# A gated Mamba and feed-forward layer on one core: a new order of five engines' work, softplus's own table, and idle transposes in the first batch

## The reference

```python
# xattn part, per batch
x  = einsum('bld,ed->bel', ctx, in_proj_w)          # 256 channels x 256 tokens
u  = silu(causal_conv4(x, conv_w) + conv_b)
dt_low, Bm, Cm = split(einsum('bdl,ed->bel', u, x_proj_w), [8, 24])
dt = softplus(einsum('brl,dr->bdl', dt_low, dt_proj_w) + dt_proj_b)
A  = -exp(A_log)                                     # 256 channels x 16 states
for each token: state = state * exp(dt * A) + (dt * u) * B;  y = state . C
y  = (y + D * u) * silu(layernorm(x_in))
x1 = x_in + tanh(g_xattn) * y
# ffn part
xq  = quant_int8(layernorm(x1));  a, b = split(xq @ w13.T)   # 704 each
g   = relu(a)**2 * b;  inner = rmsnorm(g) * norm_w
out = x1 + tanh(g_ffn) * (quant_int8(inner) @ w2.T)
```

## Time and profile before

| | us |
|---|---|
| median of 3 runs (lowest, highest) | 194.64 (194.52, 195.98) |
| the profiled execution | 194.72 |
| its span | 192.8 |
| busy TensorE, VectorE, ScalarE, GpSimd | 165.3, 145.1, 146.8, 109.9 |

### The profile page before, as it was taken

One profiled execution on the slowest core, in us unless ns is written; L12 is line 12 of the kernel. 1 busy time (PEld: TensorE's weight loads), 2 busy tenths in 40 slices (PEclk: granted clock), 3 DMA queues, 4 the chain that ended last, 5 costly groups with the idle time before them and its releaser, 6 DMA issues.

```text
span 192.8 us, 3064 instructions
## 1 busy us (share of the span) xinstructions
PE 165.3 (86%) x1010; PEld 128.1 (66%) x1010; DVE 145.1 (75%) x210; ACT 146.8 (76%) x342; POOL 109.9 (57%) x72
## 2 busy tenths in 40 slices
...
GB/s 123 368 39 202 370 336 12 212 335 58 159 6 129 201 87 188 242 256 21 67 309 247 137 7 178 39 114 0 0 2 29 0 3 0 31 0 27 27 57 55
DMA packets 21745, 22.54 MB, mean 117 GB/s; under 512 B 13337, under 2 KB 14818, under 8 KB 21602
## 3 DMA queue, kind: packets, MB, share of 16 engines
...
HBM read 19.09 MB, written 3.26 MB: 116 GB/s over the span
## 4 chain that ended last, share of the span: by engine, by line
PE 56%; DVE 21%; ACT 11%; issue 9%; DMA 2%; DVEq 0%; ACTq 0%
PE m_ps L844 18%; PE w_ps L898 11%; PE y_ps L868 10%; DVE hb L697 9%; PE w_ps L912 8%; DVE xc L642 4%; DVE fam L727 3%; ACT dA L509 2%; ACT sz L497 2%; PE w_ps L803 2%; DMA ctxT<-in_ctxT 2%; PE w_ps L825 1%; PE w_ps L905 1%; ACT xq L548 1%; DVE xstat L621 1%
## 5 line engine op out<-in xcount | busy, mean ns | idle before, releaser
L341 POOL TENSOR_TENSOR hb<-hb,cs 128x1024 f32<-128x1024 f32 x31 | 72.6, 2364 | 22.7 <-DVE hb L697 22.3
L697 DVE TENSOR_TENSOR_SCAN hb<-dA,m_ps 128x1024 f32<-128x1024 f32 x32 | 72.1, 2275 | 17.6 <-PE m_ps L844 5.8
L844 PE MATMUL m_ps<-bd,duT 128*128 128x256 f32 (+1 forms) x224 | 62.7, 422 | 9.3 <-issue 9.3
L509 ACT ACTIVATE dA<-dt,nega 128x255 f32<-128x255 f32 (+1 forms) x160 | 58.9, 451 | 5.2 <-DVE hb L697 5.2
L844 PEld LDWEIGHTS m_ps<-bd,duT 128*128 128x128 f32 x224 | 41.5, 195 | 23.1 <-issue 17.6
L868 PE MATMUL y_ps<-identf,hb 128*128 128x128 f32 x256 | 32.8, 278 | 0.0
L898 PE MATMUL w_ps<-wparts,xqT 128*128 128x352 bf16 x192 | 30.8, 313 | 1.4 <-DVE ffn L740 1.4
L868 PEld LDWEIGHTS y_ps<-identf,hb 128*128 128x128 f32 x256 | 29.7, 143 | 2.5 <-issue 1.4
L898 PEld LDWEIGHTS w_ps<-wparts,xqT 128*128 128x128 bf16 x192 | 18.5, 98 | 12.3 <-DVE ffn L740 1.9
L355 POOL TENSOR_TENSOR ffn<-ffn,normw 128x704 f32<-128x704 f32 x7 | 11.8, 1680 | 23.8 <-DVE ffn L740 23.8
L642 DVE SCALAR_TENSOR_TENSOR xc<-w_ps,sm,xc 128x255 f32<-128x255 f32 (+2 forms) x24 | 11.1, 478 | 7.7 <-ACT xc L474 7.1
...
## 6 DMA issues: line engine op xcount, KB each, us to landing
cs<-c_rows SPq DMA_DIRECT2D x16, 512.0 KB, 5.7
bd<-b_diag SPq DMA_DIRECT2D x12, 512.0 KB, 4.8
...
x<-in_x SPq DMA_DIRECT2D x1, 1024.0 KB, 8.2
...
```

Of the source, the lines that this page charges most:

```text
L341: E.tensor_tensor(h_g, h_g, cs[:, s0:s0 + sn, l0:l0 + ln], ALU.mult).then_inc(hc_end if (b, i, h) == OUT_END else hc_ok[h], 1)
L509: last = act_fn(dA_g[:, s, 1:ln], dt[:, b, h, l0 + 1:l0 + ln], ACT.Exp, scale=nega[:, h, s0 + s:s0 + s + 1])
L697: V.tensor_tensor_scan(hb[:, k % 3, h], dA[:, k % 2, h].rearrange("p n l -> p (n l)"), m_ps[:, h], 0.0, ALU.mult, ALU.add).then_inc(scan_o ...
L844: last = T.matmul(m_q[:, :, c * P - l0:(c + 1) * P - l0], duT[:, p, c, h * P:(h + 1) * P], bd[:, (s0 + sn // 2 * q) // GN, c, n0:n0 + sn / ...
```

## The change

Three things. `WARM` gets two more runs of eight transposes, and `PLAN` now uses six `warm` steps instead of one: one before the first product, four between the products of batch 0 up to `bT`, one ahead of the first `mix`. `TABLES` names `softplus` where it named `softplus_and_others`. And all five lists of `PLAN` have another order; the steps in them, apart from `warm`, are the same.

```diff
-WARM = (10, 8, 8, 8)
+WARM = (10, 8, 8, 8, 8, 8)
...
-TABLES = ("silu_and_others", "softplus_and_others", "natural_log_exp_and_others", "silu_and_others",
-          "softplus_and_others", "natural_log_exp_and_others")
+TABLES = ("silu_and_others", "softplus", "natural_log_exp_and_others", "silu_and_others",
+          "softplus", "natural_log_exp_and_others")
...
-        inproj/0.0 inproj/0.1 inproj/1.0 warm/0.0 xdbl/0.0 bT/0.0 skip/0.0 dtproj/0.0 dtproj/0.1 duT/0.0 duT/0.1
+        warm/0.1 inproj/0.0 inproj/0.1 inproj/1.0 warm/0.0 xdbl/0.0 warm/0.2 dtproj/0.0 warm/0.3 dtproj/0.1 warm/0.4
+        bT/0.0 xdbl/1.0 duT/0.0 warm/0.5 mix0/0.0 duT/0.1 mix1/0.0 bT/0.1 inproj/2.0 mix0/0.1 inproj/3.0 mix1/0.1
...
-        tap/0.0 tap/0.1 tab/0.0 tap/1.0 u/0.0 u/0.1 gates/0.0 w_hi/0.0 w_hi/0.1 u/1.0 tab/0.1 soft/0.0 soft/0.1
+        tab/0.0 tap/0.0 tap/0.1 tap/1.0 u/0.0 w_hi/0.0 u/0.1 gates/0.0 w_hi/0.1 u/1.0 tab/0.1 soft/0.0 soft/0.1
...
-        conv/0.0 conv/0.1 conv/1.0 lowc/0.0 bd/0.0 du/0.0 du/0.1 xstat/0.0 lowc/1.0 scan1/0.0 scan0/0.0 bd/0.1
+        conv/0.0 conv/0.1 conv/1.0 lowc/0.0 xstat/0.0 du/0.0 bd/0.0 du/0.1 xmr/0.0 lowc/1.0 scan0/0.0 scan1/0.0 bd/0.1
...
-        l_ctx/0.0 l_w/0.0 l_x/0.0 cput/0.0 l_w/0.1 cget/0.0 cget/0.1 dzero/0.0 cget/0.2 cput/1.0 bput/1.0 cget/0.3
+        l_ctx/0.0 l_w/0.0 l_x/0.0 l_w/0.1 cput/0.0 cget/0.0 dzero/0.0 cget/0.1 cput/1.0 cget/0.2 bput/1.0 l_w/0.2
```

More of the change, by code:

```diff
@@ L73 @@
[L73 to L77, removed]
@@ L78 @@
-        up/3.2 iqT/2.0 up/3.3 iqT/2.1 down/2.0 iqT/3.0 down/2.1 iqT/3.1 down/3.0 down/3.1
+        warm/0.1 inproj/0.0 inproj/0.1 inproj/1.0 warm/0.0 xdbl/0.0 warm/0.2 dtproj/0.0 warm/0.3 dtproj/0.1 warm/0.4
+        bT/0.0 xdbl/1.0 duT/0.0 warm/0.5 mix0/0.0 duT/0.1 mix1/0.0 bT/0.1 inproj/2.0 mix0/0.1 inproj/3.0 mix1/0.1
+        skip/0.0 mix0/0.2 sum1/0.0 sum0/0.0 sum0/0.1 mix1/0.2 mix0/0.3 sum1/0.1 xdbl/2.0 mix1/0.3 sum0/0.2 dtproj/1.0
+        xdbl/3.0 dtproj/2.0 dtproj/3.0 szT/0.0 duT/1.0 sum1/0.2 mix0/1.0 duT/2.0 mix1/1.0 sum0/0.3 szT/1.0 mix0/1.1
@@ L79 @@
+        skip/3.1 up/2.1 sum0/3.2 up/2.2 sum1/3.2 up/2.3 xqT/3.0 sum0/3.3 sum1/3.3 up/3.0 down/0.0 iqT/1.0 up/3.1
+        iqT/1.1 down/0.1 down/1.0 xqT/3.1 down/1.1 iqT/2.0 up/3.2 up/3.3 iqT/2.1 down/2.0 iqT/3.0 down/2.1 iqT/3.1
+        down/3.0 down/3.1
     """,
     "act": """
-        tap/0.0 tap/0.1 tab/0.0 tap/1.0 u/0.0 u/0.1 gates/0.0 w_hi/0.0 w_hi/0.1 u/1.0 tab/0.1 soft/0.0 soft/0.1
-        tab/0.2 nega/0.0 duT/0.0 w_mid/0.0 duT/0.1 w_hi/0.2 decay1/0.0 decay0/0.0 decay1/0.1 tap/2.0 decay1/0.2
@@ L83 @@
-        decay0/0.1 xrs/0.0 decay1/0.3 w_hi/0.3 decay0/0.2 decay0/0.3 tap/3.0 tab/0.3 u/2.0 z/0.0 z/1.0 z/2.0 z/3.0
-        u/3.0 tab/0.4 soft/1.0 w_mid/0.1 w_mid/0.2 szT/0.0 soft/2.0 soft/3.0 duT/1.0 tab/0.5 decay0/1.0 decay1/1.0
-        decay0/1.1 decay1/1.1 decay0/1.2 decay0/1.3 w_mid/0.3 szT/1.0 xn/0.0 decay1/1.2 decay1/1.3 rs1/0.0 szT/2.0
-        w_hi/0.4 quant1/0.0 w_hi/0.5 duT/2.0 decay1/2.0 decay0/2.0 w_mid/0.4 decay0/2.1 xqT/0.0 decay1/2.1 edge/3.0
-        duT/3.0 w_mid/0.5 decay0/2.2 decay1/2.2 decay1/2.3 decay0/2.3 relu/0.0 relu/0.1 decay0/3.0 rs1/1.0 xn/1.0
@@ L93 @@
-        relu/3.3 quant2/3.0 square/3.1 iqT/2.1 rs2/3.1 iqT/3.0 quant2/3.1 iqT/3.1
+        tab/0.0 tap/0.0 tap/0.1 tap/1.0 u/0.0 w_hi/0.0 u/0.1 gates/0.0 w_hi/0.1 u/1.0 tab/0.1 soft/0.0 soft/0.1
+        tab/0.2 w_mid/0.0 duT/0.0 nega/0.0 xrs/0.0 decay0/0.0 w_hi/0.2 duT/0.1 decay1/0.0 decay0/0.1 tap/2.0
+        decay0/0.2 w_mid/0.1 decay1/0.1 w_hi/0.3 decay0/0.3 w_mid/0.2 decay1/0.2 decay1/0.3 tap/3.0 tab/0.3 u/2.0
+        w_mid/0.3 z/0.0 z/1.0 z/2.0 z/3.0 u/3.0 tab/0.4 soft/1.0 w_hi/0.4 soft/2.0 soft/3.0 duT/1.0 tab/0.5 decay0/1.0
```

57 lines of the change are left out of this document (31 added, 26 removed).

## The result

The changed kernel takes **174.92 us** (median of 4 runs, 174.31 to 176.82) against 194.94 for the kernel before beside it: ratio 0.898, 95% interval 0.890 to 0.906. The forecast was 182.9 with a range of 176 to 190. The direction was right, the size was 8 us short, and the time lies 1.1 us under the range. The profiled execution took 174.31 us for a span of 172.5, where the forecast has 181.0.

The account below looks back on a forecast made before the run. Bound by a chain of hand-overs first, by TensorE's own work from the first `up`: 90.5 + 79.2 + 6.2 + 2.5 = 178.4 for the last matmul, tail 2.6, span 181.0, 1.92 around it: 182.9 us, range 176 to 190.

Parts of the forecast that it names:

- Tables: ScalarE: three table loads go, one ahead of the first product and the second of each softplus pair, 3.8 us.
- xmr: VectorE step moved ahead of the scans: 1.0 us alone instead of 4.6 beside GpSimd; ScalarE's wait, about 5.4 us, goes.
- First batch: Walk up to the first scan of batch 1: at 52.9 us instead of 63.3, a lead of 10.4 us.
- ballast: Rival: TensorE's clock stays low up to the first scans and the idle transposes cost time: 189 us, chance 0.08.
- To the first `up`: From batch 1's first scan VectorE is the chain, 35.9 us, then a 1.73 us mix: first `up` at 90.5, before 101.8.
- the neighbour rule: GpSimd shares SBUF interfaces with VectorE: a VectorE operation is long beside GpSimd work, short only while GpSimd rests.
- From there TensorE: From the first `up` at 90.5: 79.2 us of TensorE work, 6.2 gaps, 2.5 new gap; last matmul at 178.4.
- `fam/1.0`: VectorE step in the last part, waiting for a ScalarE step now queued behind a decay: a new gap, about 2.5 us.
- The opening of the prediction: What bounds the kernel: first part a chain of hand-overs, last part TensorE's own work, where reordering only moves the start.
- Tail and overhead: After the last matmul: final step and store 2.6 us, span 181.0; 1.92 us around the span.
- the lead is partly given back: Rival: in TensorE's last part VectorE and ScalarE wait on each other more, twice the gaps: 189 us, chance 0.20.
- Better: Rival: TensorE's own gaps close too, 176 to 178 us, chance 0.07.

Follow-up runs that it names:

- the second, 175.94: The changed kernel itself, unchanged, run again on the next chip beside a version with two idle transpose runs less: 175.94 us, ratio 0.900.

## Why the prediction was right and wrong, step by step

- *Tables*: six loads of 1.28 and none beside a softplus, as forecast. But 3.8 us are not a term of a sum: 0 to 1.5 in the old order, and about 3.9 for two of the three loads in the new one, of which 2.0 is pauses and clock. Counting them on top of `xmr` came out for this kernel because I walked the queue, and would have been wrong in the old order.
- *xmr*: 1.0 us, no wait of `z`. Right, bound and reason (late beside GpSimd 2.28 for one operation, alone 0.17).
- *First batch*: wrong by 2.1 us in one place, the clock. I priced the idle runs at no cost and at no gain. About 1 us is the rise at 6 us instead of 12.5, which not every execution has, and about 1 is that the clock no longer falls again before the first `mix`. My rival "ballast" had the sign reversed.
- *To the first `up`*: the engine was misnamed. I made VectorE the chain with 35.9 us and `fam` at its old 4.4. `fam` took 1.3 because GpSimd rests at 76.4 (with a GpSimd product beside it, 3.2 and the forecast's middle), and then TensorE's own 35.6 us decides. I had used the neighbour rule for `xmr` and did not ask it again for `fam`.
- ***From there TensorE*: the step that failed.** The work was about right (79.2 counted, 80.3 busy). The pauses were not: 6.2 carried over from the order before plus 2.5 for `fam/1.0` made 8.7, and 3.1 were measured. These 5.6 us too much have three parts. 2.5 is `fam/1.0`: it held VectorE 3.49 us at the place I named, yet taking that wait away changes nothing. 1.6 is an error of the sum: the 6.2 is the difference between a sum of step prices and a window, and the window's own idle time was 88.40 - 83.78 = 4.6. 1.5 is the carrying over itself: the lists joined in halves show pauses of 4.6 us with the old order behind `mix0/1.0` and 3.2 with the new one, early or late. The opening of the prediction, that a reordering can only move the start of this part, fails with it.
- *Tail and overhead*: 2.7 and 1.8 against 2.6 and 1.9. (The last sum gives 182.8, not 182.9.) The first median lies 0.6 above the profiled execution, and the second, 175.94, only 0.1 below the range: a us of the distance is chance.
- *Rivals*: "the lead is partly given back" is refuted, since lateness or lead passes through the new later half unchanged (middle 35.6 to 36.4, last part 83.3 to 83.4 in the changed kernel and four variants of it whose first scans lie between 50.8 and 60.1). "Better", TensorE's gaps close, was the true case; I gave it 0.07 and 176 to 178, without the clock and without `fam/0.0`.
